# Attention and Winograd convolution on one core: prob x val in bursts of four key chunks

## Chip, cores and metric

One core of a Trainium2 chip. The metric is the device time of one execution in microseconds. The median of three runs of the kernel before is 2642.56 us (2641.87, 2642.56 and 2645.37).

## What is computed

The input x has 8 images of 512 channels and 32 x 32 positions. Two layers with residual sums follow one another; the first one matters here:

```
t = group_norm(x), as 1024 tokens of 512 channels
q, k, v = t @ Wq.T + bq, t @ Wk.T + bk, t @ Wv.T + bv
# every token is a group of its own: g runs over B * 8, and q.reshape(B * 8, S, 64)
scores = q k^T / 8, softmax over the keys, times v
x = x + result
x = x + conv3x3(relu(mask * group_norm(x))) + bias
```

The reshape does not split channels into heads. One group takes 128 tokens with all their 512 channels, which makes 1024 rows of 64. So an image has eight independent groups of attention, each with 1024 queries and 1024 keys. The second layer is a 3x3 convolution on masked, normed data, computed by a Winograd-like scheme in one dimension.

## The kernel before

**Stages.** Stage 1 does norm, projections and attention, image by image. Stage 2 does the convolution in pairs of images. Between them lies one synchronisation of banks and buffers. The change touches stage 1 alone.

**Slots and units.** `slot` on every engine handles one group of attention: a slot `s` of 0 to 7 for each image, in all 64, numbered `h`. A slot has eight units `u`, one for each chunk of 128 keys. Four slots make a half image (`HPH = 4`), `r = s % 4`. The images 0 to 6 run partly in a loop whose body covers the slots 1 to 7 and the slot 0 of the next image.

**TensorE's order in a unit** (`slot`, line 720). The order is written out by hand:

1. place "a": one max tile of the next slot (`max_tile`, line 656).
2. `scores(h, s, u, 0)`: two f16 matmuls, the main part of the scores, for the query halves e = 0 and 1 (line 683).
3. place "b": another max tile.
4. `scores(..., 1)`: two more f16 matmuls that add the low parts and the row of the shift.
5. place "c": the remaining max tiles. In slots with r < 2 and projections, in odd units, `project_qk` follows: twelve f16 matmuls (line 638) for the q or k of the next half image.
6. place "d": in slots with r = 2 and projections, in odd units, a value projection (twelve matmuls, line 648); at unit 2 the denominator item of the previous slot (`den_item`, line 672, f32); at unit 6 the shift item (line 664, f32, a transpose of the minima); in slot 1, at units 4 and 6, two small statistics matmuls (lines 250 and 252).
7. `weigh_pair`, lines 713 to 718: prob x val for two chunks, in f32. At unit 0 it takes the chunks 6 and 7 of the previous slot, at the units 2, 4 and 6 the chunks 0-1, 2-3 and 4-5 of the own slot.

A slot has projections when it prepares the next half image: all slots but r = 3, and in the last image only s = 0, 1 and 2. `more` is false for the slots 1 to 7 of the last image.

`MAX_QUOTA = [2, 3, 3, 3, 3, 2, 0, 0]` spreads the sixteen max tiles of the next slot over the units.

**Buffers and waits.**
- The scores live in three PSUM banks, in turn (`bank_turn`, line 85). Tile `2u + e` waits until the exponential of the tile three before it is done.
- Max tiles, values, denominators, shifts and statistics share a ring of three other banks (`take`). An item waits until VectorE has released the item three before it. At one place of the image, where the count of the ring wraps, items wait for the one two before.
- `prob` has eight buffers. Exponential `2u + e` on ScalarE waits until prob x val has used the buffer eight tiles ago (`pv_done`) and until the sums of VectorE and GpSimd are through with it.
- prob x val gathers in one bank. Its first chunk waits until ScalarE has evicted the previous slot.
- ScalarE's order (`slot`, line 946): the two exponentials of the unit; at unit 0 also the eviction of prob x val of the previous slot; after projections the two evacuations of q or k (lines 874 and 878); in some slots the norm of the next image or the weights of stage 2.
- VectorE's order (`slot`, line 1441): the max reductions (line 1216) at places a to c, the splits of the normed tile, `add_tile` (line 1210) for chunk `u - 1`, two moments at the units 1 and 2 of the slots 0 and 1, then the other items: value, denominator copy (line 1242), shift copy (line 1226). After these comes the split of q or k, and at unit 4 the reciprocal of the denominators.
- GpSimd adds the odd half of prob (line 1044), divides and adds the residual.
- SP sends the row of the shift into q_b (line 386) for the next slot; TensorE waits for it before step 4 of unit 0.

The slots with projections fall into two kinds in this text: full ones (r of 0 and 1, 30 of them) and part ones (r of 2, 15 of them).

Of the kernel before, what the change touches and what calls it, by code (L numbers as in the profile page):

```python
# [28 lines left out]
B, C, HW = 8, 512, 32  # L29
# [5 lines left out]
SEG = C // D  # L35
QR4 = P // 4
QN = HALF // 2
HPI = S // TOK
HPH = HALF // TOK
# [5 lines left out]
UNITS = SEG  # L45
# [52 lines left out]
def ring_items(u, nxt, prev, v_units, stat):  # L98

    first = sum(MAX_QUOTA[:u])  # L100
    tiles = [("max", first + k) for k in range(MAX_QUOTA[u])] if nxt else []
    at = {"a": tiles[0:1], "b": tiles[1:2], "c": tiles[2:]}
    at["d"] = [("value", u // 2)] if v_units and u % 2 else []
    if nxt and u == UNITS - 2:
        at["d"].append(("shift", 0))
    if u in stat:
        at["d"].append(("stat", stat.index(u)))
    if prev and u == 2:
        at["d"].append(("den", 0))
    if prev == "direct":  # L110
        at["d"] = [x for x in at["d"] if x[0] != "den"]
    return at


def stat_units(s, more):

    if more:
        return (4, 6) if s == 1 else ()
    return (3, 5) if s == 3 else ()


def den_direct(s, more):

    return not more and s >= HPH
# [5 lines left out]
def build(nc, x, wqT, wkT, wvT, chan, bv, wcu, const, out):  # L130
# [11 lines left out]
    with top:  # L142
# [76 lines left out]
        def stat_steps(cols):  # L219
            return 2 * cols, 3 * cols, 3 * cols + 3, 3 * cols + 3 + 1 + ROOT_STEPS  # L220

        _, STAT_AGG, STAT_DEV, STAT_STEPS = stat_steps(NC)
        S2_MOM, S2_AGG, S2_DEV, S2_STEPS = stat_steps(K8)

# [377 lines left out]
        def _(pe):  # L602
# [11 lines left out]
            def stat_item(img, k):  # L614
                dst = take()
                pe.wait_ge(s_stat, img * STAT_STEPS + (STAT_AGG, STAT_DEV)[k])
                statistics_sum(pe, dst, k, NC).then_inc(s1["ring_full"], 1)

            def first_pair_stat(k):
                dst = take()  # L620
                pe.wait_ge(s2["stat2_step"], (S2_AGG, S2_DEV)[k])
                statistics_sum(pe, dst, k, K8).then_inc(s1["ring_full"], 1)
# [19 lines left out]
            def project_value(t, half, g):  # L642
                pe.wait_ge(s1["xn_split"], 2 + 4 * (t + 1))
                dst = take()
                steps = [(a, b, c) for c in range(NC) for a, b in
                         ((xn_hi, w_hi), (xn_hi, w_lo), (xn_lo, w_hi))]
                for n, (a, b, c) in enumerate(steps):
                    mm = pe.matmul(dst[:], a[:, half, c, g * TOK:(g + 1) * TOK], b[:, 2, c],  # L648
                                   start=(n == 0), stop=(n == len(steps) - 1))
                mm.then_inc(s1["ring_full"], 1)  # L650

            def max_tile(s, m):

                half, tok = tokens(s)
                dst = take()
                pe.matmul(dst[:].rearrange("p (k t) -> p k t", t=TOK), q_a[half][:, m // 2, tok],  # L656
                          k_a[half][:, 4 * (m % 2):4 * (m % 2) + 4, tok],
                          start=True, stop=True).then_inc(s1["ring_full"], 1)

            def shift_item(h):  # L660

                dst = take()
                pe.wait_ge(s1["min_done"], h + 1)
                pe.matmul(dst[0:SEG, 0:TOK], nmin[:], ident, start=True, stop=True).then_inc(s1["ring_full"], 1)  # L664

            def den_item(h, par):

                dst = take()
                for e in range(2):
                    pe.wait_ge(s1[f"sum{e}"], 7 + 7 * (h + 1))  # L670
                    for k in range(2):
                        mm = pe.matmul(dst[(2 * e + k) * QR4:(2 * e + k + 1) * QR4, 0:QN], ones[:, 0:QR4],  # L672
                                       psum_acc[:, par, e, k * QN:(k + 1) * QN], start=True, stop=True)
                mm.then_inc(s1["ring_full"], 1)
# [13 lines left out]
            def sum_prob(h, kc):  # L688

                if kc == 0:  # L690
                    pe.wait_ge(s1["qk_out"], 1 + 16 * B)
                    pe.wait_ge(s1["den_out"], h)
                for e in range(2):
                    pe.wait_ge(s1["exp_done"], 4 + 16 * h + 2 * kc + e + 1)
                    for k in range(2):
                        mm = pe.matmul(qk_bank[(2 * e + k) * QR4:(2 * e + k + 1) * QR4, 0:QN], ones[:, 0:QR4],  # L696
                                       prob[:, (2 * kc + e) % 8, k * QN:(k + 1) * QN],
                                       start=(kc == 0), stop=(kc == SEG - 1))
                if kc == SEG - 1:
                    mm.then_inc(s1["den_full"], 1)  # L700

            def weigh(h, s, kc):

                if kc == 0:
                    pe.wait_ge(s1["pv_out"], h + 1)
                    pe.wait_ge(s1["value_out"], h + 1)
                for e in range(2):
                    pe.wait_ge(s1["exp_done"], 4 + 16 * h + 2 * kc + e + 1)
                    pe.matmul(pv_bank[e * D:(e + 1) * D, :], val[s // HPH][:, s % HPH, kc * D:(kc + 1) * D],  # L709
                              prob[:, (2 * kc + e) % 8], start=(kc == 0),  # L710
                              stop=(kc == SEG - 1)).then_inc(s1["pv_done"], 1)

            def weigh_pair(h, s, n, direct=False):

                for kc in (2 * n, 2 * n + 1) if direct else ():
                    sum_prob(h, kc)
                for kc in (2 * n, 2 * n + 1):
                    weigh(h, s, kc)

            def slot(img, s, prev=True, nxt=True, more=True):  # L720
                h = img * HPI + s
                t = img * 2 + s // HPH
                r = s % HPH
                proj = r < 3 and (s < HPH or more)
                for u in range(UNITS):
                    items = ring_items(u, nxt, "direct" if den_direct(s - 1, more) else prev, proj and r == 2,
                                       stat_units(s, more))

                    def run(place):
                        for kind, a in items[place]:  # L730
                            if kind == "max":
                                max_tile((s + 1) % HPI, a)
                            elif kind == "value":
                                project_value(t + 1, 1 - s // HPH, a)
                            elif kind == "stat":
                                if more:
                                    stat_item(img + 1, a)
                                else:
                                    first_pair_stat(a)
                            elif kind == "shift":  # L740
                                shift_item(h + 1)
                            else:
                                den_item(h - 1, (s - 1) % 2)
                    if u == 0 and nxt and r == 3:

                        pe.wait_ge(s1["qk_moved"], 192 * (t + 2))
                    run("a")
                    scores(h, s, u, 0)
                    run("b")
                    if u == 0:  # L750
                        pe.wait_ge(s1["shift_row"], 16 * (h + 1))
                    scores(h, s, u, 1)
                    run("c")
                    if proj and r < 2 and u % 2:
                        project_qk(t + 1, 1 - s // HPH, r, u // 2)
                    run("d")
                    if u == 0 and prev:
                        weigh_pair(h - 1, (s - 1) % HPI, SEG // 2 - 1, den_direct(s - 1, more))
                    if u >= 2 and u % 2 == 0:
                        weigh_pair(h, s, u // 2 - 1, den_direct(s, more))  # L760

            pe.sem_inc(s1["pv_done"], 8)
            pe.wait_ge(s_const, 48)
# [22 lines left out]
            slot(B - 1, 0)  # L786
            for s in range(1, HPI):
                slot(B - 1, s, nxt=s < HPI - 1, more=False)
            weigh_pair(B * HPI - 1, HPI - 1, SEG // 2 - 1, True)


            def group_sum(pair, k):
# [382 lines left out]
        def _(dve):  # L1175
# [265 lines left out]
            def slot(img, s, prev=True, nxt=True, more=True, ahead=True):  # L1441
# [4 lines left out]
                for u in range(UNITS):  # L1446
# [27 lines left out]
                    if s == 1 and u == 3 and more:  # L1474
                        aggregate()
                    items = ring_items(u, nxt, "direct" if den_direct(s - 1, more) else prev, proj and r == 2,
                                       stat_units(s, more))
                    for place in "abcd":
                        if place == "c":
# [191 lines left out]
```

## Time and profile before

| | before |
|---|---|
| median of three runs | 2642.56 us |
| profiled execution, its own time | 2640.12 us |
| its span, first to last instruction | 2638.3 us |
| mean granted TensorE clock | 0.990 |
| TensorE busy (matmuls) | 2530.4 us |
| VectorE busy | 1952.4 us |
| ScalarE busy | 1088.2 us |
| GpSimd busy | 1163.0 us |
| prob x val matmuls (line 709) | 501.3 us busy, 2048 records |

The profiled execution is 0.1% under the median, and 1.8 us of it lie outside the span. PE stands for the matmuls of TensorE and PEld for its weight loads, DVE for VectorE, ACT for ScalarE, POOL for GpSimd, SPq for SP's queue of DMAs. An f32 matmul leaves two records. Records of matmuls overlap, since each is given its whole latency (an f16 matmul of 512 columns 0.38 us), so their pace is read from start to start (0.22 us between f16 matmuls), and busy time alone does not tell the pace.

### The profile page before, as it was taken

How to read it: one execution, taken by the hardware profiler on the slowest of the kernel's cores; microseconds unless marked ns; L12 is line 12 of the kernel's file. 1: busy time of each engine (PE TensorE's matmuls, PEld its weight loads, DVE VectorE, ACT ScalarE, POOL GpSimd, SP SyncE). 2: the span in 40 equal slices, each digit the busy share in tenths (PEclk: the TensorE clock that was granted, in tenths of full speed). 3: DMA queues.
4: the chain of work that ended last, by engine and by line, in shares of the span. 5: the costliest groups of instructions: out<-in, count | busy, mean ns of one | idle time of the engine just before them, and what ended most of it. 6: DMA issues, size and time to landing. Idle time of an engine off the chain costs nothing.

```text
span 2638.3 us, 39624 instructions
## 1 busy us (share of the span) xinstructions
PE 2530.4 (96%) x11792; PEld 993.9 (38%) x11792; DVE 1952.4 (74%) x2624; ACT 1088.2 (41%) x1801; POOL 1163.0 (44%) x980
## 2 busy tenths in 40 slices
PE   5999999999999999999999999976999999999998
PEld 2333333333333333333333333322344444444443
DVE  5877787787787778777778878787558958968614
ACT  3455455455545545545554554453332132132100
POOL 4366466566556656655655664644103003003000
PEclk9999999999999999999999999988999999999999
DMA  5234153251423415324243340630353644743533
GB/s 154 69 85 116 62 132 84 61 133 52 124 82 96 116 45 137 90 67 121 62 121 86 96 110 20 169 108 15 140 214 137 254 172 152 268 143 128 192 117 154
DMA packets 211813, 309.00 MB, mean 117 GB/s; under 512 B 82320, under 2 KB 131600, under 8 KB 211600
## 3 DMA queue, kind: packets, MB, share of 16 engines
q1 hardware_dynamic: 211600, 306.36, 38.6%
q8 instruction: 109, 1.79, 0.3%
q14 instruction: 104, 0.85, 0.1%
HBM read 202.88 MB, written 52.69 MB: 97 GB/s over the span
## 4 chain that ended last, share of the span: by engine, by line
PE 86%; DVE 7%; issue 2%; DMA 2%; ACT 1%; POOL 1%; SPq 1%; DVEq 0%; ACTq 0%; POOLq 0%
PE bank L804 28%; PE bank L709 16%; PE bank L683 14%; PE bank L638 12%; PE bank L656 8%; PE bank L648 5%; DVE nmax L1216 2%; DVE prob_sum L1210 1%; PE bank L672 1%; DMA q_b<-shift 1%; ACT prob L887 1%; PE bank L664 1%; DVE tab_mem L1297 1%; PE bank L696 0%; DVE val L1233 0%
## 5 line engine op out<-in xcount | busy, mean ns | idle before, releaser
L1216 DVE TENSOR_REDUCE nmax<-bank 128x1 f32<-128x512 f32 x1024 | 658.6, 682 | 252.8 <-PE bank L656 245.5
L887 ACT ACTIVATE prob<-bank 128x512 f32<-128x512 f32 x1024 | 555.8, 596 | 618.2 <-PE bank L683 612.1
L804 PE MATMUL bank<-v,u_slab 128*128 128x512 f16 x3456 | 746.9, 379 | 0.0
L1044 POOL TENSOR_TENSOR prob_sum<-prob_sum,prob 128x512 f32<-128x512 f32 x360 | 522.7, 1452 | 375.7 <-ACT prob L887 374.6
L709 PE MATMUL bank<-prob,val 128*64 128x512 f32 x2048 | 501.3, 611 | 0.0
L804 PEld LDWEIGHTS bank<-v,u_slab 128*128 128x128 f16 x3456 | 338.1, 98 | 406.9 <-issue 0.8
L656 PE MATMUL bank<-k_a,q_a 128*128 128x512 f16 x1024 | 387.7, 384 | 26.9 <-DVE nmax L1216 21.2
L1210 DVE TENSOR_TENSOR prob_sum<-prob_sum,prob 128x512 f32<-128x512 f32 x360 | 358.4, 996 | 12.2 <-DVE shift L1226 8.9
L683 PE MATMUL bank<-q_a,k_a 128*128 128x512 f16 x1024 | 316.9, 383 | 16.7 <-ACT prob L887 15.1
L683 PE MATMUL bank<-q_b,k_b 128*128 128x512 f16 x1024 | 307.2, 382 | 2.3 <-DMA q_b<-shift 2.2
L709 PEld LDWEIGHTS bank<-prob,val 128*64 128x64 f32 x2048 | 125.2, 137 | 239.7 <-issue 196.0
L638 PE MATMUL bank<-xn_hi,w_hi 128*128 128x512 f16 x512 | 195.0, 381 | 13.7 <-DVE xn_lo L1195 13.7
L656 PEld LDWEIGHTS bank<-k_a,q_a 128*128 128x128 f16 x1024 | 99.9, 98 | 286.0 <-issue 89.1
L638 PE MATMUL bank<-xn_lo,w_hi 128*128 128x512 f16 x512 | 194.8, 380 | 0.0
L638 PE MATMUL bank<-xn_hi,w_lo 128*128 128x512 f16 x512 | 194.8, 380 | 0.0
L874 ACT ACTIVATE qk<-bank,prm 128x512 f32<-128x512 f32 x128 | 87.9, 687 | 229.1 <-PE bank L638 229.1
L1044 POOL TENSOR_TENSOR prob_sum<-prob 128x512 f32<-128x512 f32 x60 | 76.1, 1269 | 212.5 <-ACT prob L887 211.6
L683 PEld LDWEIGHTS bank<-q_a,k_a 128*128 128x128 f16 x1024 | 95.3, 98 | 179.0 <-ACT prob L887 70.6
L1050 POOL TENSOR_TENSOR den_sb<-pv_sb,den_sb 128x512 f32<-128x512 f32 x64 | 89.7, 1402 | 150.3 <-DMA den_sb<-recip_scratch 150.3
L231 POOL TENSOR_TENSOR rstd<-ve,fixed 128x4 f32<-128x4 f32 (+1 forms) x12 | 17.6, 1467 | 293.7 <-DVE ve L212 293.7
L1202 DVE TENSOR_TENSOR qk_lo<-qk,qk_hi 128x512 f16<-128x512 f32 x128 | 126.7, 990 | 25.9 <-ACT qk_hi L878 10.1
L683 PEld LDWEIGHTS bank<-q_b,k_b 128*128 128x128 f16 x1024 | 99.6, 98 | 121.0 <-DMA q_b<-shift 8.1
(125 smaller groups left out, 2523.2 us busy)
## 6 DMA issues: line engine op xcount, KB each, us to landing
u_slab<-u_scratch SPq DMA_DIRECT2D x72, 1024.0 KB, 5.0
tile<-x_scratch SPq DMA_DIRECT2D x34, 1024.0 KB, 7.2
xs<-x SPq DMA_DIRECT2D x28, 1024.0 KB, 5.5
u_scratch<-u_w SPq DMA_DIRECT2D x96, 192.0 KB, 2.8
q_a<-qk_hi SPq DMA_DIRECT2D x64, 256.0 KB, 4.9
den_sb<-recip_scratch SPq DMA_DIRECT2D x128, 128.0 KB, 2.9
x_scratch<-xr SPq DMA_DIRECT2D x16, 1024.0 KB, 4.4
xr<-x SPq DMA_DIRECT2D x15, 1024.0 KB, 7.7
```

The costliest lines, as they stand in the source:

```text
L638: mm = pe.matmul(dst[:], a[:, w, c, j * P:(j + 1) * P], b[:, half, c], start=(n == 0), stop=(n == len(steps) - 1))
L648: mm = pe.matmul(dst[:], a[:, half, c, g * TOK:(g + 1) * TOK], b[:, 2, c], start=(n == 0), stop=(n == len(steps) - 1))
L656: pe.matmul(dst[:].rearrange("p (k t) -> p k t", t=TOK), q_a[half][:, m // 2, tok], k_a[half][:, 4 * (m % 2):4 * (m % 2) + 4, tok], start= ...
L683: mm = pe.matmul(sc_bank[b][:].rearrange("p (j t) -> p j t", t=TOK), k_op[half][:, u, tok], q_op[half][:, e, :, tok], start=(part == 0), s ...
L709: pe.matmul(pv_bank[e * D:(e + 1) * D, :], val[s // HPH][:, s % HPH, kc * D:(kc + 1) * D], prob[:, (2 * kc + e) % 8], start=(kc == 0), sto ...
L804: mm = pe.matmul(bank_at(pos, co)[:].rearrange("p (i n) -> p i n", i=2), slab[:, l, c, co * P:(co + 1) * P], image[v][:, 2 * c:2 * c + 2, ...
L887: act.activation(prob[:, (2 * u + e) % 8], sc_bank[bank_turn(s * 16 + 2 * u + e, 16 * HPI)[0]][:], ACT.Exp, scale=float(D) ** -0.5).then_i ...
L1044: nc.gpsimd.tensor_tensor(acc, in0, prob[:, (2 * kc + 1) % 8], ALU.add).then_inc(s1["sum1"], 1)
L1050: nc.gpsimd.tensor_tensor(den_sb[:], pv_sb[:], den_sb[:], ALU.mult).then_inc(s1["o_done"], 1)
L1202: dve.tensor_tensor(qk_lo[:, which, j], qk32[:, j % 2], qk_hi[:, which, j], ALU.subtract)\
L1210: dve.tensor_tensor(acc, in0, prob[:, (2 * kc) % 8], ALU.add).then_inc(s1["sum0"], 1)
L1216: dve.tensor_reduce(nmax[:, m // 2, m % 2:m % 2 + 1], src[:], AX.X, ALU.max, negate=True)\
```

## The change

The pairs of prob x val become bursts, and a new function says which chunks are weighed after unit `u` of slot `s`. `UNITS` (8) stands for unit 0 of the next slot.

```
+def pv_burst(s, u, more):
+
+    full = s % HPH < 2 and (s < HPH or more)
+    part = s % HPH == 2 and (s < HPH or more)
+    if full:
+        return {4: (0, 1, 2, 3), UNITS: (4, 5, 6, 7)}.get(u, ())
+    if part:
+        return {4: (0, 1, 2, 3), 6: (4, 5), UNITS: (6, 7)}.get(u, ())
+    return {2: (0, 1), 4: (2, 3), 6: (4, 5), UNITS: (6, 7)}.get(u, ())
...
-            def weigh_pair(h, s, n, direct=False):
+            def weigh_burst(h, s, chunks, direct=False):
 
-                for kc in (2 * n, 2 * n + 1) if direct else ():
+                for kc in chunks if direct else ():
                     sum_prob(h, kc)
-                for kc in (2 * n, 2 * n + 1):
+                for kc in chunks:
                     weigh(h, s, kc)
...
                     if u == 0 and prev:
-                        weigh_pair(h - 1, (s - 1) % HPI, SEG // 2 - 1, den_direct(s - 1, more))
-                    if u >= 2 and u % 2 == 0:
-                        weigh_pair(h, s, u // 2 - 1, den_direct(s, more))
+                        weigh_burst(h - 1, (s - 1) % HPI, pv_burst((s - 1) % HPI, UNITS, more), den_direct(s - 1, more))
+                    weigh_burst(h, s, pv_burst(s, u, more), den_direct(s, more))
...
-            weigh_pair(B * HPI - 1, HPI - 1, SEG // 2 - 1, True)
+            weigh_burst(B * HPI - 1, HPI - 1, pv_burst(HPI - 1, UNITS, False), True)
```

The waits inside `weigh` stay as they are, and so does all code of the other engines.

## Rows read from the trace of the kernel before

**Rows 1.** The page, busy time: engine, busy us, share of the span, instructions.

```profile
PE 2530.4 (96%) x11792; PEld 993.9 (38%) x11792; DVE 1952.4 (74%) x2624; ACT 1088.2 (41%) x1801; POOL 1163.0 (44%) x980
```

**Rows 2.** Timeline of PE, one pair: start us, us, engine, line, operation.

```profile
424.32 0.38 PE L656 MATMUL bank<-k_a,q_a 128*128 128x512 f16 x1
424.63 1.94 PE L709 MATMUL bank<-prob,val 128*64 128x512 f32 x8
425.11 1.46 PE L709 MATMUL bank<-prob,val 128*64 128x512 f32 x6
...
426.50 0.39 PE L656 MATMUL bank<-k_a,q_a 128*128 128x512 f16 x1
```

**Rows 3.** Timelines of PE and ACT, s = 4, units 5 to 7.

```profile
430.40 0.59 PE L683 MATMUL bank<-q_a,k_a 128*128 128x512 f16 x2
...
431.67 1.94 PE L709 MATMUL bank<-prob,val 128*64 128x512 f32 x8
433.54 0.60 PE L683 MATMUL bank<-q_a,k_a 128*128 128x512 f16 x2
...
430.60 0.69 ACT L874 ACTIVATE qk<-bank,prm 128x512 f32<-128x512 f32 x1 [1.72 <-PE bank L638]
...
431.75 1.08 ACT L887 ACTIVATE prob<-bank 128x512 f32<-128x512 f32 x2
```

**Rows 4.** Timelines of DVE and PE, s = 6, unit 3.

```profile
479.13 1.89 DVE L1216 TENSOR_REDUCE nmax<-bank 128x1 f32<-128x512 f32 x3 [0.23 <-DVE den_sb L1242]
...
479.88 0.39 PE L648 MATMUL bank<-w_hi,xn_hi 128*128 128x512 f16 x1
```

**Rows 5.** Timeline of PE, s = 1, start of units 6 and 7.

```profile
570.94 0.59 PE L683 MATMUL bank<-q_a,k_a 128*128 128x512 f16 x2
...
574.40 0.61 PE L683 MATMUL bank<-q_a,k_a 128*128 128x512 f16 x2
```

**Rows 6.** Timelines of PE and DVE, s = 4, unit 2.

```profile
414.87 0.38 PE L656 MATMUL bank<-k_a,q_a 128*128 128x512 f16 x1
...
417.79 0.42 DVE L1242 COPY den_sb<-bank 128x256 f32<-128x256 f32 x1
```

**Rows 7.** Timelines of PE and DVE, s = 0, units 2 and 3.

```profile
524.98 0.38 PE L656 MATMUL bank<-k_a,q_a 128*128 128x512 f16 x1
...
530.33 0.38 PE L656 MATMUL bank<-k_a,q_a 128*128 128x512 f16 x1
...
529.10 0.41 DVE L1242 COPY den_sb<-bank 128x256 f32<-128x256 f32 x1
```

**Rows 8.** Timelines of PE and DVE, s = 1, units 2 to 4.

```profile
555.12 0.38 PE L656 MATMUL bank<-k_a,q_a 128*128 128x512 f16 x1
...
564.86 0.38 PE L250 MATMUL bank<-mv,cst 128*128 128x8 f32 x2
...
564.04 1.87 DVE L1216 TENSOR_REDUCE nmax<-bank 128x1 f32<-128x512 f32 x3
```

**Rows 9.** Timeline of PE, s = 6, start of unit 2, and s = 2, unit 1.

```profile
473.87 0.38 PE L656 MATMUL bank<-k_a,q_a 128*128 128x512 f16 x1
...
583.18 0.39 PE L648 MATMUL bank<-w_hi,xn_hi 128*128 128x512 f16 x1 [0.32 <-DVE nmax L1216]
```

**Rows 10.** Timelines of SP's queue and PE, the shift row and its reader.

```profile
432.08 0.71 SPq L386 DMA_DIRECT2D q_b<-shift  x1
...
437.87 0.59 PE L683 MATMUL bank<-q_b,k_b 128*128 128x512 f16 x2
...
406.01 0.73 SPq L386 DMA_DIRECT2D q_b<-shift  x1
...
408.36 0.60 PE L683 MATMUL bank<-q_b,k_b 128*128 128x512 f16 x2 [0.32 <-DMA q_b<-shift]
...
573.39 0.75 SPq L386 DMA_DIRECT2D q_b<-shift  x1
...
578.78 0.60 PE L683 MATMUL bank<-q_b,k_b 128*128 128x512 f16 x2
```

## The prediction

> **What bounds the kernel now.** I read the page first: busy time, then the chain that ended last. TensorE is busy 2530.4 us of 2638.3 [rows 1], and the chain runs through it nearly all the time. So TensorE sets the time, and only what lengthens or shortens its own sequence counts; ScalarE, VectorE and the DMAs count where TensorE has to wait for them. The change lies in the attention stage. There I read the timelines of TensorE, ScalarE, VectorE and SP's queue beside each other for one image (eight slots). In a slot with projections TensorE runs with hardly a gap. What the reader is to see in those rows is not who waits now, but how much room is left before each wait that is met today.
>
> **What the change does to TensorE's order.** Matmuls, loads, DMAs and the work of every other engine stay; only the place of the prob x val matmuls moves. In a full slot (s of 0, 1, 4, 5 with projections: 30 of them) the pair at unit 2 moves to unit 4, and the pair at unit 6 to unit 0 of the next slot. In a part slot (s of 2 and 6: 15) only the pair at unit 2 moves. That is 75 pairs merged into a neighbour. So 75 times a burst gets longer, and 75 times a pair that stood in front of other work is gone.
>
> **The longer burst.** A pair of chunks costs 1.87 us to the next score or max matmul (424.63 to 426.50). It is eight records in four steps. The first takes 0.48 us (to 425.11); of the six records from there the row gives 1.46 us with 0.592 for the last, so two steps of 0.43; 0.53 us are left for the fourth. The first and the last carry a surplus of 0.15 us together [rows 2]. Four more matmuls in the middle cost 4 x 0.43 = 1.73 us. Bounds: 1.72 by the inner steps, 1.87 if nothing is saved. I take 1.73, since the row shows two inner steps alike. 75 x 1.73 = 129.8 us are added. If the removed pairs gave back their whole 1.87, the kernel would gain 75 x 0.14 = 10.5 us. The question is what they give back.
>
> **Unit 6 to 7 of a full slot: ScalarE.** Call P the moment the projection of unit 5 is through on TensorE (430.40). Score tile 15 of unit 7 reuses the bank that exponential 12 of unit 6 reads, so its first matmul waits for that exponential. ScalarE first evacuates the projection in two steps from 430.60, and then begins exponential 12 at 431.75, P + 1.35 [rows 3]. Two exponentials take 1.08 us there and start half a microsecond apart, so one takes 0.6 and ends at P + 1.95. How sharp such a release is, another place shows: a max reduction that ends at 479.13 + 0.69 (the first of three in 1.89 us) lets TensorE start at 479.88, 0.06 us later [rows 4]. So tile 15 cannot begin before P + 2.01. Today it begins 0.22 us after 433.54, at P + 3.36, since the scores of unit 6, the shift matmul and the pair (431.67) stand before it [rows 3]. Without the pair it would be ready at 431.67 + 0.22, P + 1.49, so it waits 0.52 us. The pair gives back 3.36 - 2.01 = 1.35 us and not 1.87. In s = 1 the second statistics matmul stands there too. Its unit 6 began at 570.94 and its unit 7 at 574.40 [rows 5], so tile 15 stood at P + 3.68 and 1.67 us come back. Given back: 23 x 1.35 + 7 x 1.67 = 42.8 us. What leaving the shift matmul straight into f16 scores costs no row at full clock shows. From nothing to another 0.14 us (the surplus of a burst), it would end inside the same wait, so the sum stays.
>
> **Unit 2 to 3: VectorE.** Call U the start of unit 2's first max tile on TensorE. Unit 2 sends three max tiles and the denominator item into the ring of three banks, and max tile 10 of unit 3 needs the bank of the denominator back. With the pair gone, TensorE is there at 5.35 - 1.87 = U + 3.48. The denominator's copy on VectorE stands behind three max reductions and an add, and is followed by its release (I take 0.2 us, from the 0.23 us until VectorE's next work [rows 4]).
> - s = 4 and 5: the copy ends at 417.79 + 0.42, U = 414.87, release at U + 3.55 [rows 6]. Nearly free: 1.80 us come back. With the four full slots that have no moments or no denominator, 18 x 1.80 = 32.4 us.
> - s = 0 of images 1 to 5: two moments stand before the copy too, which ends at 529.10 + 0.41, U = 524.98, release at U + 4.7. Tile 10 stood at U + 5.35 [rows 7]. 0.65 us come back: 5 x 0.65 = 3.3 us.
> - s = 1 of images 0 to 6: the same, and at unit 4 the first statistics matmul needs the bank of max tile 11. VectorE reduces that one only after aggregate and add: 564.04 + 0.66, U = 555.12, so U + 9.6 to 9.7. It stands at U + 9.74 today [rows 8]. Nothing comes back: 7 x 0.04 = 0.3 us.
> - Part slots: a value item in unit 1 and the split of the normed tile make VectorE later still. In s = 6 (U = 473.87 [rows 9]) the value projection of unit 3 needs max tile 8 reduced, and begins at 479.88, 0.06 us after that [rows 4]: it waits for VectorE already, with the pair in place. Nothing comes back (7 slots). In s = 2 it is alike, but its wait of 0.32 us at unit 1 [rows 9] goes, because the longer burst at unit 0 lets VectorE catch up: 8 x 0.36 = 2.9 us.
>
> VectorE's own work moves with TensorE by 1.73 us in units 1 and 2, so these offsets from U hold. How exactly, no row of before can show; I allow half a microsecond either way in the 27 slots bound by VectorE, 13 us up or down.
>
> **Sum.** 129.8 - (42.8 + 32.4 + 3.3 + 0.3 + 2.9) = 129.8 - 81.7 = +48 us. The profiled execution took 2640.12 us, so 2688; the median of the three runs is 2642.56, and that with 48 gives 2690.7. I say **2690 us**, slower by 1.8%. About 0.2% (5 us) is what a measurement of this kernel can tell from no change.
>
> **What else waits.** The exponential of chunk 4 needs prob's buffer from chunk 0, now weighed at the start of the burst of unit 4, and so begins inside that burst. Its readers are score tile 11 in unit 5 and the adds, both behind the other 2.7 us of the burst. The eviction of prob x val comes 1.73 us later on ScalarE; the next first chunk is weighed only in unit 4. I cost both at nothing. The shift row is the narrow one. SP issues its DMA at 432.08 and its reader of unit 0 starts at 437.87, 5.79 us later; with 1.35 us less between them 4.44 us are left. Issue to the release of the reader took 2.35 us where the queue was free (406.01 to 408.36) and 5.39 us in s = 1 (573.39 to 578.78), where a load of x for the next image stood ahead of it [rows 10]. In s = 4 and 5 no such load stands ahead, so I take the first and no wait; in s = 0 and 1 that load waits for VectorE's reciprocal, which moves by less than the shift does, so it starts earlier against it. SP's other waits keep their order.
>
> **Rivals.**
> *Faster: the drains decide.* Entering f32 costs 0.31 us against 0.22 between f16 matmuls (424.32 to 424.63), and the burst's surplus is 0.15 [rows 2]. If both went 75 times and every pair gave back all it took, the gain would be 75 x 0.24 = 18 us, 2625; by the surplus alone 2632. The Trainium skill, TensorEngine Tiling (Array Packing), Key Properties, says that a change of tiling mode drains TensorE, and the bursts run as 128x64 tiles between 128x128 ones. By that rule alone the change should gain; rows 2 agree that there is such a cost, and it does not reach the 0.52 us of the wait. For it: the room that s = 4 and 5 have. Against it: exponential 12 cannot start before the evacuation, whatever the rest does. Chance 0.07.
> *VectorE is softer than I hold.* It may catch up where its adds escape GpSimd's, and half of its waits go: the 27 slots give back 0.9 us more each, +24 us, 2667. Chance 0.13. If they go whole, what is left is 23 x 0.38 + 7 x 0.06 - 45 x 0.14 = +3 us, 2646, within 0.2%: chance 0.04.
> *The shift row becomes late.* If it takes the 5.39 us of s = 1 everywhere, the reader of unit 0 waits 0.95 us more in 30 slots: +28, 2718 [rows 10]. It decides from 4.44 us on. With nothing given back by any pair the time would be 2772. Chance 0.08.
> The forecast itself: 0.68.
>
> **Range and chances.** 2655 to 2712: it takes in the softer VectorE, the 13 us of the adds both ways and the 10 us of the burst's upper bound. Faster 0.07, within 0.2% 0.04, slower 0.89.
>
> **What would show it.** In the profile after: bursts of sixteen records lasting 3.6 us; in unit 7 of full slots a TensorE wait of about 0.5 us for an exponential, some 23 times and a shorter one 7 times; in unit 3 of s = 0 and 1 a wait over 1 us behind VectorE; in part slots three waits in unit 3 that sum to about 1.8 us; s = 4 and 5 longer by only 0.3 us each, the part slots by 1.4 to 1.7. The convolution stage after 1885 us should keep its length. I am wrong if unit 7 begins right behind the shift matmul, or if the waits are there and the image is yet no longer than 220.9 us.

## The result and the profile after

The change makes the kernel slower. Four runs after have a median of 2684.10 us (2683.26, 2683.63, 2684.57, 2685.43), four runs before 2642.22 us; the ratio is 1.0157 [1.0139, 1.0174], +41.9 us. The profiled execution took 2683.26 us with a span of 2681.5 and a mean granted clock of 0.989, so the clock is the same. TensorE's lines of the stage lie 11 further down than before (scores L694, max tiles L667, prob x val L720), those of ScalarE and VectorE 10 (exponential L897, max reduction L1226).

The page, busy time, answers to [rows 1]:

```profile
PE 2530.0 (94%) x11792; PEld 999.4 (37%) x11792; DVE 1925.6 (72%) x2624; ACT 1090.2 (41%) x1801; POOL 1151.5 (43%) x980
```

TensorE has the same number of records and the same busy time (2530.0 against 2530.4) in a span that is 43.2 us longer. So nothing was added: TensorE waits more. For whom, the groups of its waits say. The first fence is before, the second after. The columns are what waited and for whom, then the sum in us, how often, and the longest:

```profile
PE bank L656 <- DVE nmax L1216: 21.2, 27, 5.7
PE bank L683 <- ACT prob L887: 15.1, 30, 3.3
```

```profile
PE bank L667 <- DVE nmax L1226: 25.4, 32, 5.7
PE bank L694 <- ACT prob L897: 23.5, 53, 3.3
PE bank L667 <- DVEq L1254: 22.8, 28, 1.0
...
PE bank L659 <- DVE nmax L1226: 7.1, 15, 0.5
...
PE bank L261 <- DVE nmax L1226: 4.2, 7, 0.6
...
PE bank L694 <- DMA q_b<-shift: 0.4, 1, 0.4
```

The new ones are those that were forecast. Score tiles wait for an exponential 23 times more often. L1254 is the release behind the denominator's copy: 28 waits, 22.8 us, none before. The value projection (L659) waits in every part slot, and the statistics (L261) in seven slots of s = 1. The shift row waits once, for 0.4 us.

TensorE's timeline in s = 4, units 2 to 7, shows the burst and the exponential's wait:

```profile
422.18 0.38 PE L667 MATMUL bank<-k_a,q_a 128*128 128x512 f16 x1
...
425.67 0.38 PE L667 MATMUL bank<-k_a,q_a 128*128 128x512 f16 x1
...
430.08 3.65 PE L720 MATMUL bank<-prob,val 128*64 128x512 f32 x16
433.66 0.39 PE L667 MATMUL bank<-k_a,q_a 128*128 128x512 f16 x1
...
437.56 0.59 PE L694 MATMUL bank<-q_a,k_a 128*128 128x512 f16 x2
437.99 0.59 PE L694 MATMUL bank<-q_b,k_b 128*128 128x512 f16 x2
438.51 0.39 PE L675 MATMUL bank<-cst,nmin 128*8 128x128 f32 x2
438.83 0.39 PE L694 MATMUL bank<-q_a,k_a 128*128 128x512 f16 x1
439.57 0.39 PE L694 MATMUL bank<-q_a,k_a 128*128 128x512 f16 x1 [0.34 <-ACT prob L897]
```

Sixteen records take 3.58 us (430.08 to 433.66), so two merged pairs save 2 x 1.87 - 3.58 = 0.16 us of surplus; 3.60 was forecast. The projection is through at P = 437.56, and tile 15 begins at 439.57, P + 2.01, to the hundredth where [rows 3] put it. The 0.34 us in the row is counted from the end of the record before it, which is given 0.39 us. At the pace of 0.22 us from start to start the delay is 439.57 - 438.83 - 0.22 = 0.52 us, as forecast. U is 422.18; max tile 10 of unit 3 begins at 425.67, U + 3.49, with no wait.

Where VectorE has more in front of the copy, the same place looks like this (s = 1, units 2 to 4, then unit 7; TensorE's timeline):

```profile
566.24 0.38 PE L667 MATMUL bank<-k_a,q_a 128*128 128x512 f16 x1
...
570.88 0.39 PE L667 MATMUL bank<-k_a,q_a 128*128 128x512 f16 x1 [0.99 <-DVEq L1254]
...
575.98 0.38 PE L261 MATMUL bank<-mv,cst 128*128 128x8 f32 x2 [0.61 <-DVE nmax L1226]
...
585.29 0.88 PE L694 MATMUL bank<-q_a,k_a 128*128 128x512 f16 x2
```

Max tile 10 comes at U + 4.64 (forecast 4.7), the statistics at U + 9.74, which is where they stood before [rows 8]. All that the missing pair could give back is gone by then. VectorE's timeline there shows why the copy comes late:

```profile
566.65 1.99 DVE L1226 TENSOR_REDUCE nmax<-bank 128x1 f32<-128x512 f32 x3 [0.92 <-PE bank L667]
568.56 0.68 DVE L1220 TENSOR_TENSOR prob_sum<-prob 128x512 f32<-128x512 f32 x1
569.16 1.28 DVE L205 BATCH_NORM_STATS2 bn<-xs 128x6 f32<-128x512 f32 x2
570.35 0.41 DVE L1252 COPY den_sb<-bank 128x256 f32<-128x256 f32 x1
```

Two moments, 1.28 us together, stand between the add and the copy. In a part slot (s = 6) three waits follow each other, with 0.33 + 0.64 + 0.47 = 1.44 us of idle time in the rows:

```profile
481.62 0.38 PE L667 MATMUL bank<-k_a,q_a 128*128 128x512 f16 x1
...
485.29 0.39 PE L667 MATMUL bank<-k_a,q_a 128*128 128x512 f16 x1 [0.33 <-DVE nmax L1226]
...
486.75 0.39 PE L667 MATMUL bank<-k_a,q_a 128*128 128x512 f16 x1 [0.64 <-DVEq L1254]
487.62 0.39 PE L659 MATMUL bank<-w_hi,xn_hi 128*128 128x512 f16 x1 [0.47 <-DVE nmax L1226]
```

The value projection begins at U + 6.00, U + 6.01 before (479.88 - 473.87, [rows 9] and [rows 4]). Without waits TensorE would be there at 6.01 - 1.87 = U + 4.14. So counted by starts the three waits hold it up by 1.86 us.

**Slot by slot.** From one shift matmul (unit 6) to the next is one interval; I name it by the slot in which it ends. Sums over the images 0 to 6, against before, worked out from the two timelines of TensorE:

| interval ends in | after - before | forecast |
|---|---|---|
| s = 0 | +5.7 | +5.3 |
| s = 1 | +15.6 | +14.5 |
| s = 2 | +7.5 | +10.0 |
| s = 3 and 7 | 0.0 | 0 |
| s = 4 | -1.3 | -0.5 |
| s = 5 | +1.6 | +2.2 |
| s = 6 | +14.1 | +14.8 |
| last image | +0.8 | +2.0 |
| up to the first shift | -0.9 | 0 |
| sum | +43.0 | +48 |

From the last shift matmul to the end it is 789.0 us before and 789.2 after: the convolution stage kept its length.

### The profile page after: what moved, and what is told of

It reads as the page before. It is cut to its first block, busy times and chain, and to the rows that moved or that the text cites. A ratio compares the mean times of both kernels' runs of the same rounds, so it can differ in the third digit from the quotient of the medians.

```text
span 2681.5 us, 39648 instructions
## 1 busy us (share of the span) xinstructions
PE 2530.0 (94%) x11792; PEld 999.4 (37%) x11792; DVE 1925.6 (72%) x2624; ACT 1090.2 (41%) x1801; POOL 1151.5 (43%) x980
## 4 chain that ended last, share of the span: by engine, by line
PE 84%; DVE 8%; issue 4%; ACT 2%; POOL 1%; DMA 1%; SPq 0%; DVEq 0%; ACTq 0%; POOLq 0%
PE bank L814 28%; PE bank L720 17%; PE bank L694 13%; PE bank L649 12%; PE bank L667 7%; PE bank L659 6%; DVE nmax L1226 3%; ACT prob L897 2%; DVE prob_sum L1220 1%; DVE bn L205 1%; PE bank L683 1%; DVE tab_mem L1307 1%; PE bank L707 0%; DVE xn_lo L1205 0%; PE bank L675 0%
## 5 line engine op out<-in xcount | busy, mean ns | idle before, releaser
L1226 DVE TENSOR_REDUCE nmax<-bank 128x1 f32<-128x512 f32 x1024 | 661.8, 685 | 287.7 <-PE bank L667 281.0
L897 ACT ACTIVATE prob<-bank 128x512 f32<-128x512 f32 x1024 | 556.0, 596 | 628.9 <-PE bank L694 466.5
L1054 POOL TENSOR_TENSOR prob_sum<-prob_sum,prob 128x512 f32<-128x512 f32 x360 | 513.5, 1426 | 429.5 <-ACT prob L897 427.9
L720 PE MATMUL bank<-prob,val 128*64 128x512 f32 x2048 | 483.9, 606 | 0.0
L667 PE MATMUL bank<-k_a,q_a 128*128 128x512 f16 x1024 | 389.9, 386 | 54.9 <-DVE nmax L1226 25.4
L1220 DVE TENSOR_TENSOR prob_sum<-prob_sum,prob 128x512 f32<-128x512 f32 x360 | 339.7, 944 | 11.8 <-DVE shift L1236 8.9
L694 PE MATMUL bank<-q_a,k_a 128*128 128x512 f16 x1024 | 322.0, 384 | 25.9 <-ACT prob L897 23.5
L694 PE MATMUL bank<-q_b,k_b 128*128 128x512 f16 x1024 | 307.0, 382 | 0.5 <-DMA q_b<-shift 0.4
L720 PEld LDWEIGHTS bank<-prob,val 128*64 128x64 f32 x2048 | 131.8, 137 | 258.6 <-issue 238.4
L667 PEld LDWEIGHTS bank<-k_a,q_a 128*128 128x128 f16 x1024 | 99.8, 98 | 316.6 <-DVE nmax L1226 93.3
L694 PEld LDWEIGHTS bank<-q_a,k_a 128*128 128x128 f16 x1024 | 98.2, 99 | 177.1 <-ACT prob L897 69.7
L694 PEld LDWEIGHTS bank<-q_b,k_b 128*128 128x128 f16 x1024 | 100.2, 98 | 112.3 <-DMA q_b<-shift 2.9
L1212 DVE TENSOR_TENSOR qk_lo<-qk,qk_hi 128x512 f16<-128x512 f32 x128 | 114.1, 892 | 25.1 <-ACT qk_hi L888 9.3
L953 ACT ACTIVATE y<-bank 128x512 f32<-128x512 f32 x48 | 28.4, 597 | 254.9 <-PE bank L814 241.7
```

What stands on the lines that cost most here:

```text
L694: mm = pe.matmul(sc_bank[b][:].rearrange("p (j t) -> p j t", t=TOK), k_op[half][:, u, tok], q_op[half][:, e, :, tok], start=(part == 0), s ...
L897: act.activation(prob[:, (2 * u + e) % 8], sc_bank[bank_turn(s * 16 + 2 * u + e, 16 * HPI)[0]][:], ACT.Exp, scale=float(D) ** -0.5).then_i ...
L1054: nc.gpsimd.tensor_tensor(acc, in0, prob[:, (2 * kc + 1) % 8], ALU.add).then_inc(s1["sum1"], 1)
L1212: dve.tensor_tensor(qk_lo[:, which, j], qk32[:, j % 2], qk_hi[:, which, j], ALU.subtract)\
L1220: dve.tensor_tensor(acc, in0, prob[:, (2 * kc) % 8], ALU.add).then_inc(s1["sum0"], 1)
L1226: dve.tensor_reduce(nmax[:, m // 2, m % 2:m % 2 + 1], src[:], AX.X, ALU.max, negate=True)\
```

## The experiments

Each kernel had between 4 and 11 runs. With four runs the interval of a ratio is some 4 us to either side, so differences of a few us between two versions rest on the slot intervals of their traces. All kernels named `e1` and on are the kernel after with the edit shown, unless said otherwise. Medians are in us; a ratio is against the kernel before on the same chip. In the diffs

```
EARLY = {4: (0, 1, 2, 3), 6: (4, 5), UNITS: (6, 7)}
LATE  = {2: (0, 1), 4: (2, 3), UNITS: (4, 5, 6, 7)}
```

### e1: the late merge undone

```
-    if full:
-        return {4: (0, 1, 2, 3), UNITS: (4, 5, 6, 7)}.get(u, ())
-    if part:
+    if full or part:
         return EARLY.get(u, ())
```

> The changed kernel with the pair of unit 6 put back in the 30 full slots (they run 4-2-2 like the part slots); 45 merges are left. Lost cover: what the wait for exponential 12 costs goes, 0.37 us in 23 slots by the slot table of the two traces, and the wait of 0.32 us in unit 1 of s = 2 comes back, so 2684.1 - 9 + 2 = 2677 us, and the wait of 0.3 us for ScalarE in unit 7 is gone. Rival, a cost of every merge alike (42 us / 75 = 0.56 us each): 2642.2 + 45 x 0.56 = 2667 us. Rival, drains: fewer merges, fewer saved drains, so no lower than 2684.

Measured 2682.53, 1.0152 [1.0135, 1.0169]: 1.6 us under the change, where 7 were expected. The intervals tell both sides. Those of s = 5 and s = 6 lose 2.6 us each over seven images, as they should. Those of s = 1 and s = 2 give 2.7 us back, and s = 1 there has a wait that the kernel after does not have: score tiles of unit 1 wait 0.9 us and more for an exponential, right behind the turn of the loop (the loop's body ends with slot 0 and begins with slot 1). e8 and e11 show the same stall by itself. The medians of e1 and of the kernel after can't be told apart; what holds is the two parts, 5.2 us saved in s = 5 and 6 and 2.7 us lost in s = 1 and 2.

### e2: the late merge alone

```
     if full:
-        return {4: (0, 1, 2, 3), UNITS: (4, 5, 6, 7)}.get(u, ())
-    if part:
...
+        return LATE.get(u, ())
```

> The kernel before with only the pair of unit 6 moved to unit 0 in the 30 full slots. Lost cover: 23 x 0.37 + 7 x 0.06 = 9 us, less 8 x 0.32 = 2.6 us for the wait in unit 1 of s = 2, so 2642.2 + 6.5 = 2649 us, and score tile 15 of unit 7 starts at P + 2.01 in s = 0, 4 and 5. The same cost for every merge: 2642.2 + 30 x 0.56 = 2659 us. Drains alone: 2637 us or less.

Measured 2674.02 (2671.28 to 2677.85), 1.0124 [1.0107, 1.0141]: 25 us more than expected. The merge itself costs what was forecast, +0.37 us in each interval of s = 5 and s = 6 (2.6 us over seven images). The rest is two new stalls in the intervals of s = 1 (+14.7) and s = 2 (+12.6). TensorE's timeline at the turn of the loop and in s = 2:

```profile
556.95 0.39 PE L664 MATMUL bank<-k_a,q_a 128*128 128x512 f16 x1 [2.04 <-issue]
...
590.19 0.92 PE L691 MATMUL bank<-q_b,k_b 128*128 128x512 f16 x2 [2.04 <-DMA q_b<-shift]
```

The second is the rival of the prediction that the shift row becomes late, and SP's queue shows how:

```profile
583.09 0.38 SPq L434 DMA_DIRECT2D xs<-x  x1
583.75 0.41 SPq L423 DMA_DIRECT2D u_scratch<-u_w  x1
584.31 0.75 SPq L394 DMA_DIRECT2D q_b<-shift  x1
```

1.2 us before the shift row a load of x for the next image is issued, 1 MB. The busy time by stretches says when the 16 DMA engines are free again (the last two columns are their busy share and GB/s):

```profile
586.00:588.00 2.00, 2.00 (x10) 0.78 (x8) 0.52 (x2) 0.68 (x2) 2.00 (x2) 1.00 1.00 293
588.00:590.00 2.00, 0.14 (x1) 0.00 (x0) 2.00 (x4) 0.58 (x2) 1.69 (x5) 1.00 1.01 315
590.00:592.00 2.00, 1.81 (x6) 0.46 (x8) 0.07 (x1) 0.00 (x0) 1.76 (x5) 0.58 0.09 25
```

They are full until 590 us, and the reader of the row starts at 590.19, 5.9 us after the issue. The load itself lands 7.3 us after its issue, at 590.4. The Trainium skill, DMA: Bandwidth & Descriptors, Queues, rings and completion order, says that each DMA engine takes the descriptors of one ring in their order. The rows fit that, since both transfers come from SP's queue; whether the row waited for its turn or only for its share of full engines they do not tell.

### e9 and e10: the loads of x moved ahead

e9 is e2 with this edit of SP's program, e10 the kernel before with it. The loads go ahead of `send_sums`, whose steps wait for the reciprocal:

```
+                if s == 0 and ahead:
+                    load_x(img + 1, 1)
+                if s == 1 and more:
+                    load_x(img + 1, 2)
                 if prev:
                     send_sums(img * HPI + s - 1)
-                if s == 0 and ahead:
-                    load_x(img + 1, 1)
...
-                if s == 1 and more:
-                    load_x(img + 1, 2)
```

> The kernel of e2 (only the pair of unit 6 moved) with SP's two loads of x in s = 0 and s = 1 issued ahead of the DMAs of the denominators instead of behind them. e2 was 25 us over its expectation; its trace has 1.3 to 2.4 us of wait for the shift row in s = 1 to 2 of seven images and 2.0 to 2.5 us without a releaser where the loop turns, both just behind a 1 MB load of x. If the load is the cause, these go and what was expected of e2 is left: 2650 us. If the shift's own way (matmul, copy, issue) is too short without the pair, the waits stay: 2674 us.

> The kernel before with the same two loads issued ahead of the denominators' DMAs. If the load delays the code of the next pass and the shift row in this kernel too, 0.5 to 1.2 us go at five turns of the loop and up to 1 us in two slots of s = 1: 2637 to 2639 us. If not: 2641. If the denominators' small DMAs, now behind 1 MB, come too late for VectorE's reciprocal: slower than 2641.

e9: 2644.59, 1.0010 [1.0001, 1.0020]. It takes 29 us from e2 by moving two loads, and lies 5 us under the 2650 that were expected. The waits for the shift row fall from 13.8 us in 9 to 1.2 us in 2, and TensorE's wait at the turn from 10.8 to 5.6 us. The same place as above, TensorE of e9, and then the groups of its waits:

```profile
547.64 0.39 PE L664 MATMUL bank<-k_a,q_a 128*128 128x512 f16 x1 [1.15 <-issue]
```

```profile
PE bank L664 <- issue: 5.6, 5, 1.3
...
PE bank L691 <- DMA q_b<-shift: 1.2, 2, 0.8
```

So the thirty late merges, with the load out of their way, cost some 4 us against e10, and the excess of e2 was a matter of when 1 MB is fetched. Not all of the wait at the turn was: TensorE still waits 1.02 to 1.32 us at each of the five turns of e9, though no load is in flight there (before the one at 547.64 the DMA engines are 0.07 busy from 544 to 546 us and 0.02 from 546 to 548). In e10, with the pair of unit 6 in its place, it waits 0.32 us at most. e1, which also has that pair and the load where it was, waits 0.57 us at most. So the pair covers the turn of the loop as well, a place that the prediction did not count. e10: 2640.26, 0.9992 [0.9983, 1.0001], no difference that can be told, and no sign of the 2 to 5 us that were hoped for. Its waits at the turn do go, from 0.40 to 1.17 us in the kernel before to 0.32 at most; the intervals of s = 1 fall by 1.9 us in sum, and those of s = 2 and 3 rise by 1.2.

### e12: the change with the loads moved

The same edit of SP's program on the kernel after.

> The changed kernel with the same two loads issued early. Its waits behind VectorE and ScalarE stay (lost cover), the 0.6 to 1.1 us at five turns of the loop go: 2680 us. If most of the 42 us came from the loads of x after all, far lower, toward 2650.

Measured 2683.28, 1.0162 [1.0147, 1.0178], nothing gained. The waits at the turns, which were to go, stay for the most part: 3.7 us in sum, 0.58 to 1.00 each, against 4.9 us with 0.61 to 1.22. That fits e9, for the late merge is in this kernel too. What the change costs are the waits for VectorE and ScalarE. In the kernel after, the early merge delays the shift more than the reciprocal, and opens a gap that e2 lacks: ahead of the turn into image 1's slot 1 the load is issued at 321.18 and the shift row at 324.42, 3.24 us apart, against 322.70 and 324.09, 1.39 us, in e2. It is 3.24 us in e1 and e4 too, which have the early merge in slot 0, and 1.39 in e3 and in the kernel before, which have not. What the change does early protects what it does late.

### e3, e4, e5: one kind of slot at a time

```
e3:  if part:                     return EARLY.get(u, ())
e4:  if s in (0, 1) and more:     return EARLY.get(u, ())
e5:  if s in (4, 5) and more:     return EARLY.get(u, ())
```

In each of them pairs stand in all other slots.

> The kernel before with only the pair of unit 2 moved to unit 4 in the 15 part slots. Lost cover: nothing comes back of 1.73 us in s = 6 (7 slots) and in s = 2 (8 slots, the last image less), so about 7 x 1.65 + 7 x 1.5 + 0.5 = 23 us: 2665 us, with three waits behind VectorE in unit 3. The same cost for every merge: 2642.2 + 15 x 0.56 = 2651 us. Drains alone: 2640 us.

> The kernel before with only the pair of unit 2 moved to unit 4 in s = 0 and 1 of the images 0 to 6. Lost cover: 6 x 1.0 + 7 x 1.8 = 18 us, so 2660 us, with a wait of 1.0 us in unit 3 for the denominator's bank and 0.6 us at the statistics matmul of s = 1. The same cost for every merge: 2642.2 + 14 x 0.56 = 2650 us. Drains alone: 2640 us.

> The kernel before with only the pair of unit 2 moved to unit 4 in s = 4 and 5 of the images 0 to 6 (14 merges where VectorE is not late). Lost cover: the cover is not needed there, so each merge keeps its 0.15 us of saved surplus: 2642.2 - 14 x 0.15 = 2640 us. The same cost for every merge: 2642.2 + 14 x 0.56 = 2650 us.

| kernel | median | ratio | against before | forecast of the part |
|---|---|---|---|---|
| e3, part slots | 2666.48 | 1.0090 [1.0073, 1.0107] | +24.5 | +23.1 |
| e4, s = 0 and 1 | 2659.90 | 1.0066 [1.0049, 1.0083] | +17.9 | +17.2 |
| e5, s = 4 and 5 | 2639.87 | 0.9994 [0.9985, 1.0003] | -1.3 | -1.0 |

The forecast of a part is its share of the prediction's sum: 15 x 1.73 - 2.9; 5 x 1.08 + 7 x 1.69; 14 x -0.07. The same edit, a pair moved behind the next, costs 1.6 us a slot in one place and nothing in another, and what decides is whether VectorE has room before the ring's next tile. With the 4.3 us of the late merges (e9 against e10, both with the loads moved) the parts sum to 24.5 + 17.9 - 1.3 + 4.3 = 45, against 42 for the whole.

### e6: the moments moved behind the denominator's copy

The kernel after with VectorE's two moments of the units 1 and 2 issued after the items (the value, the copy) instead of ahead of them. `(moments)` stands for the four lines that issue them:

```
-                        if place == "d" and u in (1, 2) and (s == 0 and ahead or s == 1 and more):
-                            (moments)
                         for kind, a in items[place]:
...
+                    if u in (1, 2) and (s == 0 and ahead or s == 1 and more):
+                        (moments)
```

> The changed kernel with VectorE's moments of s = 0 and 1 put behind the denominator's copy instead of ahead of it. Lost cover: the bank of the denominator comes back about 1 us sooner, so the wait of 1.0 us in unit 3 goes in 12 slots. In s = 0 that stays saved (5 or 6 us); in s = 1 the statistics matmul of unit 4 still waits for max tile 11, which VectorE reaches no sooner, so its wait grows from 0.6 to 1.6 us and nothing is saved there: 2684.1 - 5.5 = 2679 us. If the wait in unit 3 decided by itself in both: 2672 us. If it is not VectorE's order that makes it: 2684 us.

Measured 2676.90, 1.0134 [1.0118, 1.0149], 7.2 us under the change. The interval of s = 0 falls from +1.01 to -0.15 us: the wait is gone and the surplus of a burst comes out as a gain. That of s = 1 stays (+15.2 against +15.6), for its wait only moves on to the statistics. TensorE of e6, in the slot of the rows above:

```profile
574.02 0.38 PE L261 MATMUL bank<-mv,cst 128*128 128x8 f32 x2 [1.55 <-DVE nmax L1226]
```

0.99 and 0.61 us in two places have become 1.55 in one. VectorE has the same work ahead of max tile 11, whichever way round it stands.

### e7: the second evacuation between two exponentials

The kernel after, with the f16 evacuation of q or k issued behind the first exponential of the next unit and not ahead of it. `qk_high` is a new helper that holds this evacuation; it followed the other one directly:

```
                 for u in range(UNITS):
                     added = not den_direct(s - 1 + u // 4, more)
                     exp_tile(h, s, u, 0, added)
+                    if u in (2, 4, 6) and r < 2 and (s < HPH or more):
+                        qk_high(t + 1, r, u // 2 - 1)
+                    if u == 0 and r in (1, 2) and (s < HPH or more):
+                        qk_high(t + 1, r - 1, 3)
                     exp_tile(h, s, u, 1, added)
```

> The changed kernel with the second evacuation of q or k on ScalarE put behind the first exponential of the next unit instead of ahead of it. Lost cover: exponential 12 can start once its scores are through, about P + 1.0, and end at P + 1.6; tile 15, ready at P + 1.49, then waits 0.1 us and not 0.5. 23 x 0.4 = 9 us are saved: 2675 us. If the wait is due to something else than the evacuation ahead of it: 2684 us. A price on VectorE, whose split of q or k comes 0.5 us later, would show as longer waits in unit 3.

Measured 2677.41, 1.0139 [1.0124, 1.0155], 6.7 us under the change. TensorE's waits for an exponential fall from 23.5 us in 53 to 14.0 in 29, and s = 4, unit 7 has no wait:

```profile
437.54 0.39 PE L675 MATMUL bank<-cst,nmin 128*8 128x128 f32 x2
437.86 0.69 PE L694 MATMUL bank<-q_a,k_a 128*128 128x512 f16 x2
438.39 0.60 PE L694 MATMUL bank<-q_b,k_b 128*128 128x512 f16 x2
```

The intervals of s = 5 turn from +0.22 to -0.22, those of s = 6 fall by 0.44 too, and those of s = 1 keep their sum (+15.9 against +15.6), since the turn's waits grow to 1.02 to 1.52 us and those at the statistics from 4.2 to 6.2 us in sum, the price on VectorE that was named. So it was ScalarE's order ahead of exponential 12 that held tile 15, as [rows 3] were read.

### e8 and e11: only the merges that are covered

e8 makes the early merge in s = 0, 4 and 5 alone and moves the moments as e6 does; e11 adds the moved loads of x.

```
e8:  if s in (0, 4, 5) and more:  return EARLY.get(u, ())
```

> A version meant to beat both: the pair of unit 2 moved to unit 4 only in s = 0, 4 and 5 of the images 0 to 6, and VectorE's moments behind the denominator's copy, so that s = 0 has room as well. Lost cover: 20 to 21 merges keep 0.15 us each, 2642.2 - 3 = 2639 us. The same cost for every merge: 2654 us.

> The kernel of e8 with the same two loads issued early. e8 was 3.5 us over its expectation, with 1.3 to 1.5 us of wait for ScalarE's first exponential after the turn of the loop, which has no releaser itself. If that is its code coming late behind the load, it goes: 2636 us. If it stays: 2642.

e8: 2642.65, 1.0005 [0.9996, 1.0014]. e11: 2641.77, 1.0003 [0.9994, 1.0012]. e8 lies 3.7 us over its expectation, and e11 on the value that was named for the wait staying, so the load is not its cause. Nearly all of their 22 merges (s = 0 of the last image is among them) give their 0.15 us, and then the intervals of s = 1 that pass the loop's turn take 0.5 to 1.5 us each, 5 us in all. ScalarE's timeline of e11 there, and then TensorE's:

```profile
546.20 0.68 ACT L884 ACTIVATE qk_hi<-bank,prm 128x512 f16<-128x512 f32 x1
550.29 1.08 ACT L893 ACTIVATE prob<-bank 128x512 f32<-128x512 f32 x2 [3.42 <-issue]
```

```profile
545.84 0.39 PE L663 MATMUL bank<-k_a,q_a 128*128 128x512 f16 x1 [0.27 <-issue]
550.95 0.39 PE L690 MATMUL bank<-q_a,k_a 128*128 128x512 f16 x1 [1.24 <-ACT prob L893]
```

Between ScalarE's last instruction of one pass and its first of the next lie 3.42 us. Before it is 1.6 to 2.2 us in the five turns. It is 3.4 to 3.6 us in every turn of e1, e4, e8 and e11, the four kernels in which slot 0, the last of the body, has its bursts by 4, 2, 2; in the kernel after, in e3, e5, e10 and e12 it is 1.6 to 2.6. In e11 the x load is out of the way, and the gap is the same, so it is not the load. (In e2, where the load lands just as TensorE reaches the turn, the gap is 3.4 to 5.5 us; in e9, without it, 2.4 to 2.7.) Why the burst's form in slot 0 makes it longer stays open.

No kernel of the study is measurably faster than the one before.

## Why the prediction was right

The forecast was 2690 us and slower; measured 2684.1. The theory, that the pairs removed give back only what room VectorE and ScalarE leave, held in place after place.

- **The burst.** Forecast 3.60 us and 1.73 added; measured 3.58 and 1.71. "The drains decide" is out as a verdict, but its rule is at work where nothing waits: each merge in s = 4 gives 0.15 us in the profile after. I took 0.07, because the two inner steps were read as 0.43 each and the copy's release as a shade later than tile 10.
- **Unit 6 to 7.** P + 2.01, met to the hundredth, and the delay of 0.52 us with it; +0.37 us a merge in the intervals of s = 5 and 6 of e2 against 0.38. e7 shows the cause by removing it.
- **Unit 2 to 3.** U + 4.64 against 4.7; U + 9.74 against "stands at 9.74"; the part slots' three waits 1.86 us by starts against 1.8. s = 0 with moments and denominator are six slots and not five, a slip of 1 us in the count.
- **VectorE softer than held.** It did not catch up: the offsets from U moved by less than 0.1 us, and e6 shows the wait walking on when it is removed at one place.
- **The shift row.** It is not late in the kernel after. The argument in the prediction, that the load of x starts earlier against the shift, is what e2 confirms from the other side: with the late merge alone the load does stand right ahead of the row, and the reader waits 1.3 to 2.4 us in s = 2 of seven images. That and the stall at the turn make most of the 25 us. The rival was real; its condition was the gap between two issues, not the 4.44 us of room alone.

The sum was 5 us too high. Half of it (2.5 us) is s = 2: its interval costs 1.2 us and not 1.43 (in image 0 only 0.58), since it began with stalls that the change removes for nothing. The wait of 0.32 us at unit 1 is the row's idle time; from start to start the change takes 0.48 us out of that unit, where I took 0.36. In image 0 the reader of the shift row waited 1.01 us before and not after; that row was there to be read, and I costed s = 2 by one image. The last image's s = 2 is the same case: its value projection waited 1.60 us for VectorE before, so that slot lost 0.30 us where 1.7 was forecast. The 0.15 for 0.07 of s = 4 makes another 1.4 us. 0.9 us before the first shift are nothing that the change touches.

What was not foreseen is that the parts don't add: undoing the late merge was worth 1.6 us where 7 were expected (through ScalarE at the loop's turn), and doing it alone cost 32 where 6.5 were expected (through SP's queue and the turn). The prediction had no term for the turn of the loop, and that none was needed is luck: the change as a whole lengthens TensorE's waits at the five turns by only 1.3 us (4.9 against 3.6), its late half alone by 7.

## What to carry to other kernels

Where an engine runs without a gap, a block moved out of its stream gives back only the distance to the next wait that is met today, so read that distance at each place (time of the releasing instruction against the time at which the engine would be there) before counting what the merge saves: here 0.15 us saved a merge against up to 1.7 us of wait uncovered. Count the turn of a loop among these places. Ask of each part alone whether it would stand, because another part may protect it: the late merge was cheap beside the early one and cost 32 us without it. Keep large prefetches away from a small transfer that is on the path, and from the turn of a loop (moving two such loads took 29 us from e2, and nothing measurable from the kernel before).

## What was not expected of the hardware

**Code at the turn of a loop.** TensorE's first instruction of a pass waits for nothing that the profile shows. The wait is 0.40 to 1.17 us before, at most 0.32 with the x load issued earlier (e10), and 1.99 to 2.52 in e2. There TensorE is at the turn 5.1 us after the load's issue and the load lands at 5.5 us (in the kernel before TensorE is there at 6.5 us). Yet the wait lasts until 556.95 at the second turn, and from 555 to 557 us the DMA engines are 0.03 busy at most: it outlasts the load. Without the load it is 1.02 to 1.32 in e9 and 0.58 to 1.00 in e12. So the load is a part of it, and how early TensorE reaches the turn another. The kernel after has this row:

```profile
557.14 0.39 PE L667 MATMUL bank<-k_a,q_a 128*128 128x512 f16 x1 [0.81 <-issue]
```

That fits a fetch of instructions which shares the DMA engines with the data; the page lists two queues of kind instruction:

```profile
q8 instruction: 109, 1.79, 0.3%
q14 instruction: 104, 0.85, 0.1%
```

The columns are packets, MB and share. The Trainium skill, Runtime: NRT & Kernel Launch, Instruction fetch mechanics, says that a taken branch to code outside the loaded window has to fetch it by DMA before the engine goes on. That there are waits at each turn, and that they grow in e2, agree with it; that it is this fetch and nothing else was not shown, and ScalarE's 3.42 us did not follow the load.

**A row of 2 KB behind 1 MB.** The shift row takes 2.35 us where the queue is free [rows 10], 5.39 us behind the load in the kernel before [rows 10], and 5.9 us in e2, where the load lands at 590.4 and the row's reader starts at 590.19.
